# Attention, quantised matmul and residual on one core: the row maxima's lead, the order of the loads, and two transfers moved to ScalarE's queue

## The reference

```
Q, K, V = heads(Wq x), heads(Wk x), heads(Wv x)       # 16 heads of 32, 1024 positions
att = softmax over k of ((Q K^T / sqrt(32) + b) * m + (1 - m) * -1e30)
y   = (att V), back to [8, 512, 1024]
scale = max(absmax over 1024 of y, eps) / 127;  q = round(y / scale)
out = x + float16(q . weight^T * scale * w_scale + bias)
```

## Time and profile before

| What | Value |
|---|---|
| median of 3 runs | 2477.64 us |
| the profiled execution's own time | 2481.57 us |
| its span in the trace | 2479.8 us |
| mean granted TensorE clock | 0.967 of full speed |
| PE / DVE / ACT / POOL busy | 93% / 65% / 53% / 69% of the span |
| DMA queues: GpSimd's (q0) / SyncE's (q1) | 39.7% / 36.9% of the 16 engines' span |

### The profile page before, as it was taken

One profiled execution on the slowest core, in us unless ns is written; L12 is line 12 of the kernel. 1 busy time (PEld: TensorE's weight loads), 2 busy tenths in 40 slices (PEclk: granted clock), 3 DMA queues, 4 the chain that ended last, 5 costly groups with the idle time before them and its releaser, 6 DMA issues.

```text
span 2479.8 us, 34453 instructions
## 1 busy us (share of the span) xinstructions
PE 2305.8 (93%) x11856; PEld 1377.3 (56%) x11888; DVE 1613.0 (65%) x2779; ACT 1317.3 (53%) x2471; POOL 1711.6 (69%) x735
## 2 busy tenths in 40 slices
PE   8999999999998989899989889989899899998997
PEld 7888888885444445444545445444454455444543
DVE  3311111167787778777878778778778778777873
ACT  3322222216665656565656556556566556565664
POOL 3322222416878778888888878888888888888886
PEclk9999999999999999999999999999999999999999
DMA  6655555558888888888888888888888888888874
GB/s 238 250 204 187 212 200 199 170 183 173 187 188 189 184 186 192 184 184 188 185 189 182 184 181 184 188 182 184 187 185 180 187 193 192 189 182 186 190 167 105
DMA packets 150866, 464.70 MB, mean 187 GB/s; under 512 B 13688, under 2 KB 49528, under 8 KB 126400
## 3 DMA queue, kind: packets, MB, share of 16 engines
q0 software_dynamic: 27360, 199.24, 39.7%
q1 hardware_dynamic: 123360, 263.53, 36.9%
HBM read 161.51 MB, written 100.93 MB: 106 GB/s over the span
## 4 chain that ended last, share of the span: by engine, by line
PE 69%; DMA 18%; POOL 4%; issue 4%; SPq 3%; DVE 2%; ACT 0%; POOLq 0%; ACTq 0%
PE pv L812 14%; PE ring L140 13%; DMA k_stack<-bias_part 13%; PE score L786 12%; PE ring L338 10%; PE score L338 9%; DMA probs<-probs 5%; PE ring L855 4%; POOL acc L1115 3%; PE pv L338 3%; SPq L122 2%; PE ring L822 2%; SPq L128 1%; DVE half_max L147 1%; PE ring L845 1%
## 5 line engine op out<-in xcount | busy, mean ns | idle before, releaser
L147 DVE TENSOR_REDUCE half_max<-ring 128x1 f32<-128x512 f32 x2048 | 1260.4, 677 | 162.5 <-PE ring L140 158.0
L912 ACT ACTIVATE probs<-score 128x512 f32<-128x512 f32 x2039 | 1040.9, 622 | 492.9 <-PE score L786 480.5
L1115 POOL TENSOR_TENSOR acc<-acc,probs 128x2048 f32<-128x2048 f32 x189 | 911.6, 4823 | 194.9 <-DMA probs<-probs 194.8
L140 PE MATMUL ring<-k_stack,q_stack 98*128 98x512 f32 x2048 | 843.8, 412 | 140.5 <-DMA k_stack<-bias_part 112.2
L786 PE MATMUL score<-q_stack,k_stack 100*128 100x512 f32 x2039 | 849.9, 418 | 2.2 <-ACT probs L912 1.8
L140 PEld LDWEIGHTS ring<-k_stack,q_stack 98*128 98x128 f32 x2048 | 396.9, 194 | 258.8 <-DMA k_stack<-bias_part 122.6
L786 PEld LDWEIGHTS score<-q_stack,k_stack 100*128 100x128 f32 x2039 | 391.3, 192 | 250.9 <-issue 131.9
L812 PE MATMUL pv<-probs,v_in 128*32 128x512 f32 x4096 | 526.3, 634 | 0.0
L1115 POOL TENSOR_TENSOR acc<-probs 128x2048 f32<-128x2048 f32 x63 | 288.2, 4575 | 88.1 <-DMA probs<-probs 58.4
L549 POOL TENSOR_TENSOR q_stack<-x_raw,k_stack 128x1024 fp32r<-128x1024 f32 x28 | 67.8, 2448 | 293.6 <-ACT k_stack L415 293.6
L812 PEld LDWEIGHTS pv<-probs,v_in 128*32 128x32 f32 x4096 | 110.8, 113 | 254.1 <-ACT probs L912 127.2
(11 more groups left out here) (111 smaller groups left out, 1895.8 us busy)
## 6 DMA issues: line engine op xcount, KB each, us to landing
probs<-probs POOLq DMA_DIRECT2D x190, 1024.0 KB, 9.0
q_stack<-qk_part SPq DMA_DIRECT2D x192, 256.0 KB, 4.9
k_stack<-qk_part SPq DMA_DIRECT2D x96, 512.0 KB
qk_part<-part_hi SPq DMA_DIRECT2D x64, 512.0 KB, 2.7
qk_part<-part_lo SPq DMA_DIRECT2D x64, 512.0 KB, 3.6
v_steps<-v_out SPq DMA_DIRECT2D x64, 256.0 KB, 2.3
v_in<-v_steps SPq DMA_DIRECT2D x32, 512.0 KB, 19.9
v_out<-x SPq DMA_DIRECT2D x32, 512.0 KB, 4.0
```

The source lines that it names most:

```text
L140: pe.matmul(bank[:, :], q_stack[par][0:ROW_MAX, chunk, h, qt * P:(qt + 1) * P], k_stack[par][0:ROW_MAX, h, half * N:(half + 1) * N], start ...
L147: nc.vector.tensor_reduce(half_max[:, pair // CHUNK, pair % CHUNK, half:half + 1], bank[:, :], AX_X, ALU.max, negate=True).then_inc(neg_ma ...
L912: nc.scalar.activation(probs[:, kt, h, :], score[score_bank(s, t)][:, :], ACT.Exp).then_inc(exp_done, 1)
L1115: nc.gpsimd.tensor_tensor(acc[:, half, :, :], first, probs[:, tile, :, :], ALU.add).then_inc(acc_done, 1)
```

## The change

`OWN` goes from 18 to 20: the maxima of step s+1 begin at t = 20, 44 units before the step ends instead of 46. The joins move with it, to t = 19 and t = 51, the units after which the transposes are issued; the transposes stay where they are. In the projection 22 pairs of maxima (`EARLY`) are made instead of 23, and the last step makes 20 units of them instead of 18.

On SyncE's queue the two bias rows are issued ahead of the three keys. The load of V moves behind the maxima's store and the query loads, that is behind t = 19. The query loads of s+2 move ahead of the maxima's store of t = 51, so that they wait only for half of the step's scores (t = 31). The store of the second output half and the residual load leave SyncE: ScalarE issues the store after t = 51, behind its own rounding to integers and ahead of L169, and waits there for GpSimd's residual addition; it issues the load after t = 59 and waits there until both output halves are stored.

```
-OWN = 18
+OWN = 20
...
                 if ahead and not first:
                     sp.wait_ge(score_done, UNITS * s)
+                    for part in range(2):
+                        load_bias(sp, bias_d, k_stack, s + 1, 1 - par, part, k_loaded)
                     for k in range(3):
                         load_k(sp, qk_d, k_stack, s + 1, 1 - par, k, k_loaded)
-                    for part in range(2):
-                        load_bias(sp, bias_d, k_stack, s + 1, 1 - par, part, k_loaded)
                 if second:
                     store_out(s - 2, 0)
+                sp.wait_ge(max_lo_done, 2 * s + 2)
+                store_max(sp, q_stack, max_parts, par, 1, max_rows)
                 if ahead:
+                    for k in range(3):
+                        load_q(sp, qk_d, q_stack, s + 1, 1 - par, 1, k, q2_loaded)
                     if first:
                         for i in range(2):
                             sp.wait_ge(v_stored[i], 16 * B * TT // 2)
                     wait(sp, pv_done, QH * TT * s)
                     sp.dma_start(v_in[:, 1 - par, :, :], v_d[bass.ds(s + 1, 1)].rearrange("o p a c -> (o p) a c")).then_inc(v_loaded[1 - par], 16)
-                sp.wait_ge(max_lo_done, 2 * s + 2)
-                store_max(sp, q_stack, max_parts, par, 1, max_rows)
-                if ahead:
-                    for k in range(3):
-                        load_q(sp, qk_d, q_stack, s + 1, 1 - par, 1, k, q2_loaded)
-                if second:
-                    store_out(s - 2, 1)
-                    sp.wait_ge(out_stored, 32 * (s - 1))
-                if prev:
-                    sp.dma_start(res[:, :], x[bass.ds((s - 1) * P, P), :]).then_inc(res_loaded, 16)
-                if ahead:
-                    sp.wait_ge(max_lo_done, 2 * s + 3)
-                    store_max(sp, q_stack, max_parts, 1 - par, 0, max_rows)
                 if not isinstance(s, int) or s + 2 < STEPS:
                     sp.wait_ge(score_done, UNITS * s + UNITS // 2)
                     for k in range(3):
                         load_q(sp, qk_d, q_stack, s + 2, par, 0, k, q1_loaded)
+                if ahead:
+                    sp.wait_ge(max_lo_done, 2 * s + 3)
+                    store_max(sp, q_stack, max_parts, 1 - par, 0, max_rows)
...
+            def store_out(s, half):
+                act.wait_ge(res_done, 2 * s + half + 1)
+                act.dma_start(out[s * P:(s + 1) * P, half * N:(half + 1) * N],
+                              res[:, half * N:(half + 1) * N]).then_inc(out_stored, 16)
+
+            def load_res(s):
+
+                wait(act, out_stored, 32 * s)
+                act.dma_start(res[:, :], x[s * P:(s + 1) * P, :]).then_inc(res_loaded, 16)
...
                     if t == INTS and prev:
                         make_ints(s - 1)
+                        if s >= 2:
+                            store_out(s - 2, 1)
+                    if t == SUMS_0 and prev:
+                        load_res(s - 1)
                     if t == TURN_0 and ahead:
                         high_max(nc, act, ring_of(("turn", t)), max_parts, marks, s + 1, 0, maxT_done, max_rows, max_hi_done)
```

## The result

The changed kernel takes 2423.12 us (median of 4 runs, 2416.5 to 2425.76), the kernel before 2477.41 us. The ratio is 0.9775, 95% interval 0.9755 to 0.9796: faster by 54 us. Forecast were 2403 us and a range of 2365 to 2452.

What follows compares the result with a forecast made beforehand. TensorE's key wait, then GpSimd's copy-delayed chain, bound the kernel. A step of 58.1 - 1.5 + 0.6 = 57.2 us against 59.78 saves 75 us in 29 steps: 2477.6 to 2403 us, range 2365 to 2452.

Steps and rivals of the forecast that it cites:

- The limits: TensorE's key wait, 108.4 us in 26 waits, then GpSimd's chain, said to pace steps without a key wait.
- 58.1: Base step in us without key wait: seven of steps 2 to 30 waited at most 1.1 us for keys.
- I take 1.5: Two copies on GpSimd's chain land 1.5 us earlier a step, as V and queries leave the saturated stretch; bounds 0 and 3.5.
- taken 0.6: ScalarE's wait for the residual at t = 51 costs 0.6 us a step; bounds 0 and 2.5.
- Nothing on the end's path waited for them: SyncE loses its waits for residual and stored output; maxima's store and query loads stood behind; no gain counted.
- the lead (3.0 us): Two units and a burst before keys are needed: keys may land 3.0 to 3.8 us later without a wait.
- I take 2 us earlier: Bias rows issued ahead of keys: keys land 2 us earlier; bounds 5 us earlier to 2.2 us later.
- taken 0: Transposes start 0.3 us later, twice a step, behind the later join; said absorbed, bounds 0 and 0.6 us a step.
- Keys still late: Rival, chance 0.15: keys land when the bias rows did; only the two units help, 42 us gained, time 2436.
- the rule of the Trainium skill on increments: Each DMA engine's semaphore increment lands after its earlier writes; pair 2's copy would hold back keys, reordering gains nothing.
- ScalarE stands at t = 51: Rival, chance 0.06: copy of pair 1 takes 13.4 us, residual ends at 50.9, step 61.3, time 2521.
- its deciding point: Residual's end 49.4 us into a step, from which ScalarE's wait decides: 59.78 less 10.4 from residual to step's end.

Runs made afterwards that it cites:

- u_q: The changed kernel with the query loads of s+2 back behind the maxima's store of t = 51; 2395.1 us, ratio 0.9662.
- act_only: The kernel before with only the second output store and the residual load moved to ScalarE's queue; 2446.1 us, ratio 0.9874.
- u_act: The changed kernel with the second output store and the residual load back on SyncE's queue; 2433.3 us, ratio 0.9810.
- u_q_act: u_q with the second output store and residual load back on SyncE, ahead of the maxima's store of t = 51; 2430.7 us, ratio 0.9831.
- own_only: The kernel before with OWN = 20 alone; 2462.3 us, ratio 0.9935.
- u_own: The changed kernel with OWN = 18; 2426.4 us, ratio 0.9827.
- v28: u_q with the load of V made to wait for the score of t = 27; 2395.8 us, ratio 0.9674.
- the fastest kernel here: u_q with the second-half query loads of s+1 and V made to wait for the score of t = 27; 2386.0 us, ratio 0.9643.
- store_sp: u_q with the second output store on SyncE and only the residual load on ScalarE's queue; 2393.8 us, ratio 0.9669.
- u_v: The changed kernel with the load of V back ahead of the maxima's store of t = 19; 2434.7 us, ratio 0.9819.

## Why the prediction came out as it did

**The limits were read rightly.** The key wait went, GpSimd's chain became the limit, a step fell to 57.85 where 57.2 was forecast. The time of 2423 lies in the range and 20 us above the forecast; 0.65 x 29 = 19 us of that is the step.

**The base less the copies earlier, "58.1" and "I take 1.5".** The copy of pair 2 lands 1.0 us earlier (20.5 to 19.5 us after a step's start, medians), that of pair 0 1.4 (26.7 to 25.3). The two terms can be measured together in u_q, where ScalarE doesn't wait for the residual: a step of 1651.6 / 29 = 56.95 us, 1.15 below the 58.1 of the seven steps, where 1.5 was taken.

**ScalarE's wait, "taken 0.6".** ScalarE stands 43.5 us for the residual, in 17 of 29 steps. Its price, with all else that the late copy does, is the difference to u_q: 57.85 - 56.95 = 0.9 us a step, 28 us of the medians. The wait was named; its price was too low, since it leaves out the slower matmuls behind it (17.5 of 26.1 us are busy time of TensorE). Its cause was half named: the copy of pair 1 is late by the query loads at t = 32 only with V under way beside them. By this reckoning the two terms, 0.35 and 0.3 us off, are the whole miss of 0.65.

**"Nothing on the end's path waited for them" was wrong.** That sentence, on what stood behind SyncE's waits for the residual and the stored output, is the step that failed. The query loads of s+2 stood there, and when they start decides when the keys land. Moving the two transfers alone brings the keys from 18.8 to 16.2 and gives 30 us (act_only). The four combinations, all with the lead, the bias rows first and the late V:

| Query loads of s+2 | Two transfers on | Kernel | Keys landed | Key wait us | Median us |
|---|---|---|---|---|---|
| t = 32 | ScalarE | changed | 14.4 | 1.0 | 2423.1 |
| t = 32 | SyncE | u_act | 16.2 | 3.1 | 2433.3 |
| last | ScalarE | u_q | 14.8 | 4.2 | 2395.1 |
| last | SyncE | u_q_act | 19.3 | 49.1 | 2430.7 |

The query loads get out of the keys' way by their own move or by that of the two transfers ahead of them. Either ends most of the wait; with neither 49.1 us stay. The forecast credited the missing key wait to the lead (3.0 us) and to the bias order (2 us). The lead alone halves the wait (own_only), but all parts without the lead leave only 11.5 us of it (u_own), so it is not what the wait went by. The forecast's sum holds because it only needed the wait to be gone, not why: the query loads were moved for the copies' sake, and that this ended the key wait too was in part luck.

**The bias rows, "I take 2 us earlier".** Keys land 0.6 us earlier by the order (14.4 against 15.0), and 1.1 in u_q (14.8 against 15.9). They weren't late because the bias rows stood last. Still the order is worth 12 to 22 us, by a way that stays open.

**The transposes, "taken 0".** TensorE waits 11.9 us in 46 places for the join, 0.26 us each, as worked out (0.3). u_own, without it, isn't faster, so it was absorbed.

**The rivals.** "Keys still late" didn't come: the keys land at 14.4, 5 us before the copy of pair 2. No row shows whether a write of that copy stood ahead of the keys' last increments, so the rule of the Trainium skill on increments, quoted in the forecast, is neither confirmed nor refuted here. "ScalarE stands at t = 51" came in part, at 0.9 us a step and below its deciding point: the residual of step 5 ends at 47.1 after the step's start, not at 49.4 (median 46.9; one of 29 steps, with 49.6, is over 49). It ends there with a step of 59.4, though, 12.3 us later, where the forecast had counted 10.4. A part of the difference is TensorE's slow clock behind its wait: the matmuls shown take 0.63 where 0.40 is usual.

**The range and the signs.** The bounds named for the range (copies 0 to 3.5 us earlier, wait 0 to 2.5) add up to a step of 54.6 to 60.6, not 56 to 59; the range was drawn narrower than its own terms. Of the signs, the key wait and the step came as said. The copy of pair 2 took 12.6 us (by 12 was said), the share in the third quarter rose to 1.01 (about 0.8 was said), and ScalarE's wait was 1.5 us a step (under 1 was said). One sign of being wrong did come: TensorE waits longer for the sums, 14.1 us against 6.9. It was a bad sign to choose, for in u_q, 28 us faster, this wait is longer still:

```profile
PE ring L816 <- POOL acc L1123: 20.6, 27, 1.5
```

The wait tells that GpSimd's chain is the limit, not that the kernel got slower.

## What to carry to other kernels

A wait in an issuing queue delays every transfer behind it, and these then collide with what comes next; look for it when a transfer is late, before its own size and place. A load moved out of a saturated stretch pays only if no accumulating copy with a consumer close behind runs in the new place: the third quarter had a share of 0.51, and 768 KB there, beside V's 512 KB, still cost 28 us. A wait is paid for by the engine's slower matmuls behind it as well as by its own length. An edit that is to move a load must be seen to move it: v28's wait moved V by 0.4 us. And a change with a right sum can have a wrong account: undo the parts one by one (the fastest kernel here, 0.9643, has one of the moves taken back).

## What the runs showed of the hardware

The Trainium skill's "DMA: Bandwidth & Descriptors", section "Issuing engines are not separate DMA queues", says that issuing from several engines only saves the sequencer's time to start a transfer. By the rows that time is 0.34 us for the residual load. These runs show more: moving the two transfers to ScalarE was worth 36 us (u_q against u_q_act), about 1.2 us a step. SyncE's wait in front of the load, 5.4 us in the step shown, no longer held back the loads behind it, which started 48.0 instead of 54.2 us into a step. With the load alone moved the time is the same (store_sp).

The 1 MB copy with accumulation took 7.0 us at the median in the third quarter of a step, 7.5 with 768 KB of query loads issued 2 to 3 us ahead of it (u_v), 9.5 with V under way too (changed), and 12.3 to 14.3 in the first 30 us of a step.

A pair of bias transfers of 16 KB each, put ahead of the keys instead of behind them, was worth 12 and 22 us in two surroundings with at most 4.3 us of key wait either way. This was not expected and not explained.
